# A four-stage graph kernel: eight blocks of layer 2 kept in SBUF, the weight split moved, and rings for the marks and results of the last stage

## The reference, cut to what matters

```python
def _L0_gnn_ref(x, edge_index, edge_attr, bases, W_pre, b_pre, W1, b1, g1, be1, W2, b2, g2, be2):
    edge_feat = gelu((x[src_idx] + edge_attr) @ W_pre + b_pre) * bases
    y = x + segment_sum(edge_feat, dst_idx, num_segments=N)
    h = maximum(_bn(y @ W1 + b1, g1, be1), 0.0)      # statistics over all 50,000 rows
    h = maximum(_bn(h @ W2 + b2, g2, be2), 0.0)
    return y + h
def _L1_gnn_ref(feat, src, dst, rel, ...):
    S = feat[src]
    msgs = edge_nn(S, W_rel[rel], b_rel[rel])        # relu, twice the same weights
    agg = segment_sum(msgs, dst, num_segments=n_nodes)
    # then gates (sigmoid, tanh, sigmoid) and three dense layers on agg
x = _layernorm(x + _L0_gnn_ref(...))
return _layernorm(x + _L1_gnn_ref(x, ...))
```

## Time and profile before

| | us |
|---|---|
| median of three runs (lowest, highest) | 2051.4 (2044.15, 2055.25) |
| profiled execution | 2051.5 |
| its span, first to last instruction | 2049.7 |
| PE / DVE / ACT / POOL busy | 1797.7 / 1604.4 / 1298.1 / 1074.7 |

### The profile page before, as it was taken

One profiled execution on the slowest core, in us unless ns is written; L12 is line 12 of the kernel. 1 busy time (PEld: TensorE's weight loads), 2 busy tenths in 40 slices (PEclk: granted clock), 3 DMA queues, 4 the chain that ended last, 5 costly groups with the idle time before them and its releaser, 6 DMA issues. The chain is left out here.

```text
span 2049.7 us, 27458 instructions
## 1 busy us (share of the span) xinstructions
PE 1797.7 (88%) x8697; PEld 1401.3 (68%) x8697; DVE 1604.4 (78%) x2326; ACT 1298.1 (63%) x1818; POOL 1074.7 (52%) x1200
## 2 busy tenths in 40 slices
PE   4577589999998889998999999955999999999994
PEld 3465468888886566675666666634887888888883
DVE  4688456767667889996999999984787888888883
ACT  2334346666656788886788888862665666666663
POOL 7456546767706820000555656557787764444443
PEclk9899799999999999999999999987999999999997
DMA  9999999999997999998999999965555422222210
GB/s 351 360 356 396 356 358 337 337 343 330 339 303 199 340 360 325 337 321 318 351 386 386 388 388 383 392 254 161 160 159 170 124 80 69 69 71 74 65 42 28
DMA packets 194033, 541.42 MB, mean 264 GB/s; under 512 B 27013, under 2 KB 77295, under 8 KB 193506
## 3 DMA queue, kind: packets, MB, share of 16 engines
q1 hardware_dynamic: 136354, 414.86, 55.4%
q0 software_dynamic: 47136, 73.62, 15.6%
q10 hardware_dynamic: 10400, 51.20, 6.5%
HBM read 341.49 MB, written 253.66 MB: 290 GB/s over the span
## 5 line engine op out<-in xcount | busy, mean ns | idle before, releaser
L616 POOL DMA_INDIRECT scratch_y<-sums,k_target x196 | 315.2, 1608 | 159.8 <-issue 72.4
L1005 ACT ACTIVATE d_o<-d_u,d_free 128x256 f32<-128x256 f32 x392 | 203.2, 589 | 66.3 <-POOL d_free L1042 66.3
L978 PE MATMUL d_pN<-d_y,d_free 128*128 128x512 f32 x392 | 193.3, 616 | 43.0 <-DVE d_u L1068 34.0
L983 PEld LDWEIGHTS d_pN<-k_ident,d_r 128*128 128x128 f32 x1568 | 191.5, 193 | 47.3 <-issue 46.8
L58 PE MATMUL pU<-d_part_h,k_w_h 128*128 128x512 f32 x392 | 166.3, 424 | 38.5 <-DVE d_part_l L860 17.1
L983 PE MATMUL d_pN<-k_ident,d_r 128*128 128x128 f32 x1568 | 191.6, 276 | 0.0
L848 DVE TENSOR_TENSOR d_part_l<-pT,d_part_h 128x1024 fp32r<-128x1024 f32 x98 | 119.9, 1224 | 86.0 <-ACT d_part_h L795 86.0
L795 ACT ACTIVATE d_part_h<-pT 128x1024 fp32r<-128x1024 f32 x98 | 100.5, 1026 | 132.1 <-PE pT L767 118.4
L58 PE MATMUL pS<-d_part_h,k_w_h 128*128 128x512 f32 x392 | 165.5, 422 | 15.3 <-ACT d_h L817 9.2
L1039 POOL TENSOR_TENSOR d_free<-d_free,k_minus_half 128x8 f32<-128x8 f32 (+1 forms) x100 | 163.7, 1637 | 0.2
L1068 DVE SCALAR_TENSOR_TENSOR d_u<-d_pN,d_free,k_base 128x256 f32<-128x256 f32 x392 | 161.1, 474 | 0.0
(11 more groups left out here) (219 smaller groups left out, 4946.3 us busy)
## 6 DMA issues: line engine op xcount, KB each, us to landing
scratch_h<-d_h SPq DMA_DIRECT2D x192, 512.0 KB, 7.7
out<-d_o SPq DMA_DIRECT2D x97, 520.0 KB, 5.9
k_ring<-scratch_y SPq DMA_DIRECT2D x98, 512.0 KB, 7.7
d_h<-scratch_h SPq DMA_DIRECT2D x98, 512.0 KB, 7.0
d_y<-scratch_y SPq DMA_DIRECT2D x98, 512.0 KB, 7.8
scratch_y<-in_x ACTq DMA_DIRECT2D x25, 2000.0 KB, 19.7
k_ring<-scratch_h SPq DMA_DIRECT2D x94, 512.0 KB, 5.6
attr<-in_attr_t SPq DMA_DIRECT2D x25, 512.0 KB, 15.2
```

The costliest lines, as they stand in the source:

```text
L616: pool.indirect_dma_start(out=A["y"], out_offset=bass.IndirectOffsetOnAxis(ap=K.target[:, t:t + 1], axis=0), in_=K.sums[:, t], in_offset=N ...
L978: pe.matmul(pN[k % 4][:, 2 * two:2 * two + 2].rearrange("p j f -> p (j f)"), twice[:], y[:, k % 4, two * 2 * F:(two + 1) * 2 * F], start=T ...
L983: last = pe.matmul(pN[k % 4][:, j, cc * P:(cc + 1) * P], r[:, k % 4, cc, j * P:(j + 1) * P], K.ident[:], start=False, stop=j % 2 == 1 and ...
L1005: last = act.activation(o[:, k % 4, j, 0:F], u[:, k % 3, j], ACT.Identity, bias=nb[:, n, j:j + 1], scale=rs[:, n, J + j:J + j + 1])
```

## The change

- The last KEPT = 8 blocks of layer 2 (86 to 93) are not stored to h2: four stay in `held`, four in the first ring of stage three. Before the fifth, ScalarE waits until all take-backs have ended. Stage three takes these eight first, in a new `order`, without h2 loads; the others follow, 97 last as before.
- Since `held` is in use then, the load of the raw weights goes into the middle of stage three (SP, k = 49), and VectorE's split behind its last statistics and GpSimd's last root.
- Stage four: `cont` is loaded per block into a ring of four, `has` gets a fourth place; results are held for eight blocks instead of six (`HELD` of `edges1`), so that the first store comes at step 8; from step 2 on two picks a step instead of three, ending at step 7, and at most two stores a step instead of three.

```diff
-HELD = 4
+HELD, KEPT = 4, 8
...
-    store_of: object
+    held: object
+    kept: list
...
-    stores = [g for g, (layer, k) in enumerate(passes) if layer == 2 or k < NB - HELD]
+    stores = [g for g, (layer, k) in enumerate(passes) if (g < 2 * NB - KEPT if layer == 2 else k < NB - HELD)]
...
-        return held[:, k - (NB - HELD)] if g not in store_no else h[:, store_no[g] % 4]
+        if g in store_no:
+            return h[:, store_no[g] % 4]
+        if layer == 1:
+            return held[:, k - (NB - HELD)]
+        n = g - (2 * NB - KEPT)
+        return held[:, n] if n < HELD else K.shared_sums[0][:, n - HELD]
...
+            if g == 2 * NB - KEPT + HELD:
+                for q in range(4):
+                    act.wait_ge(halved_in[q], 16 * ((ET - 1 - q) // 4 + 1))
...
-    return SecondStage(stored, halved_in, h_done, coef2_ready, coef2_pool, len(stores), lambda k: store_no[NB + HELD + k])
+    return SecondStage(stored, halved_in, h_done, coef2_ready, coef2_pool, len(stores), held, [k for _, k in passes[2 * NB - KEPT:]])
...
+    order = second.kept + [k for k in range(NB) if k not in second.kept]
...
-            if k >= 4:
+            if k >= KEPT:
-            else:
-                n = second.store_of(k)
-                sp.wait_ge(second.stored[n % 4], 16 * (n // 4 + 1))
-            sp.dma_start(h2[:, k % 4], A["h2"][k]).then_inc(h2_full[k % 4], 16)
+                sp.dma_start(h2[:, k % 4], A["h2"][order[k]]).then_inc(h2_full[k % 4], 16)
-            sp.dma_start(y[:, k % 4], rows(k)).then_inc(y_full[k % 4], 16)
+            sp.dma_start(y[:, k % 4], rows(order[k])).then_inc(y_full[k % 4], 16)
-            some = slice(S.dup if k == NB - 1 else 0, P)
-            sp.dma_start(out_rows(k)[some], o[some, k % 4].rearrange("p j f -> p (j f)")).then_inc(o_out[k % 4], 16)
+            some = slice(S.dup if order[k] == NB - 1 else 0, P)
+            sp.dma_start(out_rows(order[k])[some], o[some, k % 4].rearrange("p j f -> p (j f)")).then_inc(o_out[k % 4], 16)
-        for k in range(2):
-            load(k)
-        sp.dma_start(raw_wl[:], A["wt"]).then_inc(wl_full, 16)
-        for k in range(2, 4):
+        for k in range(4):
+            if k == NB // 2:
+                sp.dma_start(raw_wl[:], A["wt"]).then_inc(wl_full, 16)
...
-            act.wait_ge(h2_full[k % 4], 16 * (k // 4 + 1))
+            if k >= KEPT:
+                act.wait_ge(h2_full[k % 4], 16 * ((k - KEPT) // 4 + 1))
+            else:
+                act.wait_ge(second.h_done, 2 * NB - KEPT + k + 1)
+            block_k = second.held[:, k] if k < HELD else h2[:, k % 4]
-                last = act.activation(r[:, k % 4, cc], h2[:, k % 4, cc * B:(cc + 1) * B], ACT.Relu,
+                last = act.activation(r[:, k % 4, cc], block_k[:, cc * B:(cc + 1) * B], ACT.Relu,
...
-        dve.wait_ge(wl_full, 16)
-        dve.tensor_copy(K.wl_h[:], raw_wl[:]).then_inc(wl_split, 1)
-        dve.wait_ge(wl_split, 1)
-        dve.tensor_tensor(out=K.wl_l[:], in0=raw_wl[:], in1=K.wl_h[:].bitcast(F32), op=ALU.subtract)
+        dve.wait_ge(root_kept, NB)
+        dve.wait_ge(wl_full, 16)
+        dve.tensor_copy(K.wl_h[:], raw_wl[:]).then_inc(wl_split, 1)
+        dve.wait_ge(wl_split, 1)
+        dve.tensor_tensor(out=K.wl_l[:], in0=raw_wl[:], in1=K.wl_h[:].bitcast(F32), op=ALU.subtract)
...
-        HELD = 6
+        HELD = 8
-        cont, has = sb("e1_cont", [P, S.TC * P], U8), sb("e1_has", [P, 3, 2, B], U8)
+        cont, has = sb("e1_cont", [P, 4, B], U8), sb("e1_has", [P, 4, 2, B], U8)
...
-        has_full, marks = [sem(f"has_full{b}") for b in range(3)], sem("marks")
+        has_full, cont_full = ([sem(f"{n}{b}") for b in range(4)] for n in ("has_full", "cont_full"))
...
-            first = 7 + 3 * k
-            return list(range(first, min(first + 3, EB))) if k >= -1 else []
+            first = 7 + 3 * k if k < 2 else 9 + 2 * k
+            return list(range(first, min(first + (3 if k < 2 else 2), EB))) if k >= -1 else []
...
-                if k >= 3:
-                    sp.wait_ge(hid_done, C * 2 * (k - 2))
+                if k >= 4:
+                    sp.wait_ge(hid_done, C * 2 * (k - 3))
+                    sp.wait_ge(summed, C * (k - 3))
-                sp.dma_start(has[:, k % 3], one.to_broadcast([P, 2, B])).then_inc(has_full[k % 3], 16)
+                sp.dma_start(has[:, k % 4], one.to_broadcast([P, 2, B])).then_inc(has_full[k % 4], 16)
+                line = A["cont"][k * B:k * B + tiles(k) * P].rearrange("(a e) -> a e", a=1)
+                sp.dma_start(cont[:, k % 4, wide(k)], line.to_broadcast([P, tiles(k) * P])).then_inc(cont_full[k % 4], 16)
...
-            line = A["cont"].rearrange("(a e) -> a e", a=1)
-            sp.dma_start(cont[:], line.to_broadcast([P, S.TC * P])).then_inc(marks, 16)
...
-                    for _ in range(3):
+                    for _ in range(2):
...
-                dve.wait_ge(has_full[k % 3], 16 * (k // 3 + 1))
+                dve.wait_ge(has_full[k % 4], 16 * (k // 4 + 1))
-                                         in1=has[:, k % 3, r, wide(k)], op0=ALU.max, op1=ALU.mult).then_inc(hid_done, 1)
+                                         in1=has[:, k % 4, r, wide(k)], op0=ALU.max, op1=ALU.mult).then_inc(hid_done, 1)
-                dve.wait_ge(marks, 16)
+                dve.wait_ge(cont_full[k % 4], 16 * (k // 4 + 1))
-                dve.tensor_tensor_scan(msg[:, k % 2, cc, wide(k)], cont[:, k * B:k * B + tiles(k) * P], msg[:, k % 2, cc, wide(k)], start,
+                dve.tensor_tensor_scan(msg[:, k % 2, cc, wide(k)], cont[:, k % 4, wide(k)], msg[:, k % 2, cc, wide(k)], start,
```

## The result

| | before | after |
|---|---|---|
| median of six runs, us | 2049.56 | 2034.57 |
| lowest, highest | 2044.15, 2055.25 | 2029.97, 2039.01 |
| profiled execution, its span | 2051.5, 2049.7 | 2029.97, 2028.2 |

A forecast was written before the change was run, and what follows sets the result against it. The prediction took VectorE to bound stage three and TensorE steady stage four, with the change acting at both seams and stage four's early steps. Terms: -5.4 + 1.0 + 0.8 - 2.8 - 6.9 = -13.3; 2051.5 - 13.3 = 2038.2 us, range 2030 to 2047.

The forecast's parts named there:

- Layer 2's end: End of layer 2: dropping eight 512 KB stores gains nothing, and ScalarE's new wait for the halved rows costs nothing: 0.
- Seam to stage three: From layer 2's coefficients to stage three's first scaling: 5.4 us gained, TensorE late next; bounds 1.3 and 7.8.
- rival 1: The clock keeps its level at the seam to stage three and the weights' load is absorbed: 2034.8 us; 14 in 100.
- First steps of stage three: Eight h2 loads (11.0 us of DMA time) fall away while VectorE sets the pace: 0.
- rival 2: Stage three is bound by DMA after all, so each load taken away counts, 11.0 us more: 2027 us; 5 in 100.
- Weights' load in the middle: Middle of stage three: 4.3 us of transfers delay h2 and y loads, VectorE stalls 1.0 us; bounds 0 and 4.3.
- Rival 4: The weights' load tips stage three's loop of store, load, Relu and copy into slower steps: 2063 us; 5 in 100.
- Seam to stage four: End of stage three: the split makes VectorE last at the barrier, 0.8 us lost; 0 to 3.4.
- Start of stage four: First gathers no longer share DMA with the 1600 KB of marks: 2.8 us gained; bounds 0 and 3.0.
- GpSimd's picks: Stage four, steps 1 to 4: fewer picks make GpSimd early from step 3 on, 6.9 us gained; bounds 4.1 and 6.9.
- Rival 3: The seams give back half: first gathers slow by themselves, 4.3 us in the middle, 3.4 at the end: 2046.9; 22 in 100.
- 5: Rival: the change does nothing at stage four's picks, GpSimd's lateness coming from waits for moved blocks: 2045.1 us; 4 in 100.

The follow-up runs named there:

- kept4: The changed kernel with four kept blocks instead of eight, so four more stores and h2 loads: 2036.00 us, one run.
- split_longer: The changed kernel with one more VectorE subtraction (3.5 us) ahead of the weights' split at the end of stage three: 2037.84 us, one run.
- y_first_wl_early: The changed kernel with y parts of blocks 0 to 3 ahead of all transposes and the weights' load ahead of the seam: 2030.23 us, ratio to before 0.9891.
- the two groups marked: Two of three experiment groups, where every kernel took some 40 us longer: the kernel before has medians 2097.41 and 2087.45 there, 2053.12 in the third.
- control: The changed kernel itself, measured again in one of the two groups marked *: 2072.04 us, ratio to the kernel before 0.9920.

## Why the prediction was right

The time was 3.6 us below the forecast. Of these, 1.9 are the kernel before, whose median of six runs is 2049.56 where the forecast set out from 2051.5; the change itself was forecast at -13.3 us and is -15.0 by the medians. The sign and the order of the terms held:

- Layer 2's end, 0: not contradicted. ScalarE has no wait for a store or for the halved rows between 850 and 954 us after the change, but the scatter of that stretch (above) would hide some us.
- Seam to stage three, -5.4 (bounds 1.3 and 7.8): measured -6.4. TensorE was next and its clock did fall, as forecast, but not when forecast: it was 1.00 through the whole idle time and fell some 0.35 us behind the restart. The argument against rival 1, that the fall comes ahead of the restart, is refuted. What was mis-sized is the time at the lower level: I had 8.1 us from block 0's first transpose to the end of block 1 (2.7, 3.5 and 1.95); it took 958.48 + 1.95 - 953.24 = 7.2. Two errors stand against each other in it. The 2.69 us that I read as the price of 16 transposes at the lower level are a mixture, since the clock of before was 0.50 in 964 to 966 us but 0.99 in 966 to 968; nearly all at the lower level they cost 3.51. And the clock was back for most of the next y part (2.10 and not 3.5), since the lower level ended near 957; before, windows of 2 us show it from 956 to 966 us. The lower bound, 1.3, was measured by moving the split alone (one run).
- First steps of stage three, 0: right (kept4). That refutes rival 2, stage three as DMA's.
- Weights' load in the middle, +1.0: +1.1 in the profile after and again when it is taken out. The mechanism is right: the h2 wait forecast at 3.7 us was 3.23, and VectorE stalled 0.9 us in two places. The size was partly luck: over eight profiles the load costs 0.3 to 3.0 us. Rival 4, the loop that tips, did not come: the queue drained, since the step that waits also issues late.
- Seam to stage four, +0.8: measured 0.0. VectorE's end was forecast within 0.1 us relative to the root, but the cover reached 0.6 us past it and not 0.7 short of it, as split_longer shows. The forecast gave the last store's landing and VectorE the same way to the first issue. By the rows that isn't so: 2.7 us lie between the store's landing (1381.4) and the first issue before, but 1.4 behind VectorE's end in split_longer. By this difference VectorE may end 1.3 us behind the landing unseen, and it ended 0.8 behind it (1371.6 against 1368.19 + 2.6); the 0.5 left is an estimate that fits the 0.6 measured.
- Start of stage four, -2.8: measured -2.5; the fourth gather took 3.3 us, not 2.8, with the three smaller loads ahead of it. The 25 small loads of marks cost nothing that shows later: TensorE is busy for 434.2 of 437.0 us in 1553 to 1990 us, at a DMA share of 0.29.
- GpSimd's picks, -6.9: measured -6.9.

The sum of these terms, -13.3 in the forecast, is -14.7 in the traces, and -16.2 with the 0.4 us of the next stretch and the 1.1 us of the tail. For the tail I have no cause; it is 484.7 to 485.9 us in the four unmarked profiles with the changed last stage, so its scatter is as large. By its number rival 1 (2034.8) came nearer to the measured 2034.57 than the forecast (2038.2), but by chance: both its conditions failed, since the clock fell and the weights' load was not absorbed; the seam gave 6.4 and not 7.8. Rival 3 fell with the two seams and 5 with the picks.

## What to carry to other kernels

Taking work off the engine that is last is worth only the distance to the one behind it: 5.3 us of split were worth 1.3, until transfers and TensorE's order were moved too, and the trace of before already gave that number. A gap that can't be closed (statistics to coefficients) is the place for the other engine's work that needs no coefficient: here it shortened the path and held the clock at 1.00 (y_first_wl_early). A bulk load belongs where the queue is idle; in a full queue the rings' slack hid a part of its 4.3 us that differed from run to run, and 0.3 to 3.0 us were left here.

## What the runs showed of the hardware

In the two groups marked * all kernels stall at the start of stage four: 48 to 56 us between the transposes of blocks 1 and 2, where the unmarked runs take 21 to 22. In control, waits between 1384 and 1445 us:

```profile
ACT e_hidp_h L1423 <- issue: 16.0, 2, 8.9
...
PE pR L58 <- issue: 15.3, 2, 14.0
...
DVE e_hid L1518 <- remote: 13.6, 3, 6.4
```

Three engines wait in the same stretch for nothing that the profile names ("remote" is a releaser that it doesn't know), while GpSimd issues a gather about every 1.3 us. It came in all seven profiles of the marked groups and in none of the six others. The record has chip 8 both with it and without it, so it doesn't go with the chip's number; its cause is open, and no run was made for it. It is worth some 30 us, more than the change, and the spread of the runs there hides gains of several us in the medians.
